# Attention weights and their x in float16 halves, and transposes moved from TensorE to transposing DMAs

## The reference

```
x = x + layernorm(attn(layernorm(x), W_qkv, W_out))
x = x + layernorm(ffn(layernorm(x), w_gate_up, w_proj))

attn:  qkv = x @ W_qkv.T                       # W_qkv 1536 x 512, 16 heads of 32
       q, k = phi(q), phi(k)                   # phi(x) = elu(x) + 1
       out = q * cumsum(k * v) / (q * cumsum(k) + 1e-9)   # elementwise, along the tokens
       return out @ W_out.T * 32 ** -0.5       # W_out 512 x 512
ffn:   weights rounded to scale * {-1, 0, 1} in groups of 64 (4096 x 512 and 512 x 2048)
       gate, up = split(x @ wq_gu.T);  h = silu(gate) * up
       return rms_norm(h) @ wq_p.T
```

## Time and profile before

| | us |
|---|---|
| median of 2 runs (1126.14 and 1129.27) | 1127.7 |
| span of the profiled execution | 1126.3 |
| PE busy in it | 1090.9 (97%) |
| DVE busy | 759.4 (67%) |
| POOL busy | 518.8 (46%) |
| ACT busy | 465.2 (41%) |

### The profile page before, as it was taken

One profiled execution on the slowest core, in us unless ns is written; L12 is line 12 of the kernel. 1 busy time (PEld: TensorE's weight loads), 2 busy tenths in 40 slices (PEclk: granted clock), 3 DMA queues, 4 the chain that ended last, 5 costly groups with the idle time before them and its releaser, 6 DMA issues. The chain is left out here.

```text
span 1126.3 us, 14647 instructions
## 1 busy us (share of the span) xinstructions
PE 1090.9 (97%) x5376; PEld 656.7 (58%) x5376; DVE 759.4 (67%) x1220; ACT 465.2 (41%) x788; POOL 518.8 (46%) x474
## 2 busy tenths in 40 slices
PE   7998889999999999999999999999999999999997
PEld 6876455554566864468544774458644685544443
DVE  5999989875678697448862588427873479445323
ACT  5546576664522134422443224432444234423433
POOL 1567687987352444425424254414344254234322
PEclk9998999999999999999999999999999999999999
DMA  7021333110030210002100210002100020100101
GB/s 273 17 75 39 112 107 118 57 29 1 1 113 1 75 38 1 1 1 75 38 1 1 76 38 1 1 1 75 38 1 1 1 75 1 38 1 1 38 1 38
DMA packets 29256, 44.99 MB, mean 40 GB/s; under 512 B 1536, under 2 KB 9728, under 8 KB 29184
## 3 DMA queue, kind: packets, MB, share of 16 engines
q1 hardware_dynamic: 29184, 44.05, 12.2%
HBM read 34.60 MB, written 9.44 MB: 39 GB/s over the span
## 5 line engine op out<-in xcount | busy, mean ns | idle before, releaser
L546 PE MATMUL bank<-x3t,wgu_t 128*128 128x512 f16 x1536 | 348.6, 381 | 2.2 <-ACT ht L952 1.6
L546 PEld LDWEIGHTS bank<-x3t,wgu_t 128*128 128x128 bf16 x1536 | 149.1, 98 | 181.2 <-issue 4.3
L1287 POOL TENSOR_TENSOR acc<-acc,ht 128x512 f32<-128x512 f32 x90 | 114.6, 1274 | 252.0 <-ACT ht L993 251.1
L582 PE MATMUL bank<-wproj_t,hid 128*128 128x512 bf16 x872 | 203.4, 379 | 1.7 <-ACT wproj_t L873 1.7
L1658 DVE TENSOR_TENSOR ht<-ht,bank 128x512 f32<-128x512 f32 x112 | 76.0, 678 | 141.6 <-PE bank L546 124.6
L527 PE MATMUL bank<-xnt,wqkv_hi 128*128 128x512 f32 x672 | 168.0, 392 | 0.0
L582 PEld LDWEIGHTS bank<-wproj_t,hid 128*128 128x128 f16 x872 | 85.1, 98 | 102.1 <-issue 2.6
L527 PEld LDWEIGHTS bank<-xnt,wqkv_hi 128*128 128x128 f32 x672 | 125.2, 188 | 25.9 <-issue 0.2
L980 ACT ACTIVATE hid<-ht 128x512 f16<-128x512 f32 x109 | 68.7, 630 | 164.9 <-DVE ht L1658 164.8
L1664 DVE TENSOR_TENSOR hid<-ht,hid 128x512 f16<-128x512 f32 x109 | 83.0, 761 | 65.7 <-ACT hid L980 65.2
L1233 POOL TENSOR_TENSOR tk<-tq,ts 128x512 f32<-128x512 f32 x28 | 52.4, 1871 | 125.8 <-DVE ts L1569 98.5
(11 more groups left out here) (189 smaller groups left out, 1561.0 us busy)
## 6 DMA issues: line engine op xcount, KB each, us to landing
raw_q<-in_L_ffn_w_gate_up_dram SPq DMA_DIRECT2D x32, 256.0 KB, 2.8
xn<-in_L_attn_x_dram SPq DMA_DIRECT2D x7, 1024.0 KB, 5.3
out_dram<-xn SPq DMA_DIRECT2D x7, 1024.0 KB, 8.8
x<-in_L_attn_x_dram SPq DMA_DIRECT2D x6, 1024.0 KB, 6.6
raw_q<-in_L_ffn_w_proj_dram SPq DMA_DIRECT2D x16, 256.0 KB, 2.8
raw_a<-in_L_attn_W_qkv_dram SPq DMA_DIRECT2D x12, 256.0 KB, 5.5
xn<-in_L_attn_x_dram SPq DMA_DIRECT2D x4, 256.0 KB, 3.1
raw_out<-in_L_attn_W_out_dram SPq DMA_DIRECT2D x4, 256.0 KB, 6.6
```

The lines of the kernel that those rows point to most:

```text
L546: last = pe.matmul(bank[:], wgu_t[:, k, first_row:first_row + P], x[:, part, k], start=(n == 0), stop=(n == 2 * KD - 1))
L582: last = pe.matmul(bank[:], hid_of(f, part, k)[:, t * P:(t + 1) * P], wproj_t[:, k], start=(k == 0 and part == 0), stop=(k == MT - 1 and p ...
L1287: pool.tensor_tensor(acc[:], acc[:], ht_of(f)[:, m % 2], ALU.add).then_inc(q["acc_done"], 1)
```

## The change

- `wqkv_hi`, `wqkv_lo`, `xnt` and `xnt_b` become float16. W_qkv's rows are scaled by powers of two first: DVE finds each row's largest magnitude (`weight_peak`), makes the power from it in six tiny instructions (`weight_power`: `enlarge` and its inverse `reduce`). ACT's `weight_hi` and DVE's `weight_lo` write the scaled parts in row layout (`wsplit`), and `reduce` goes as a scale into the relu, the exp and the product that read the groups' banks.
- `turn_weights`, `turn_x` and `turn_x3` on SP are transposing DMAs, SBUF to SBUF: 8 of 128x12x128 for W_qkv (hi and lo of four tiles), 2 of 128x16x128 (512 KB each, hi and lo) for x of each of the chunks 1 to 7 and for x3 of each of the 8 chunks. ACT (`x_hi`, `x3_hi`) and DVE (`x_lo`, `x3_lo`) now split `xn` itself, in row layout, into `xs` and `x3s`, ahead of the DMA.
- PE keeps the transposes of x of chunk 0 (16) and of W_out (16). 288 others go: 48 of W_qkv, 112 of x, 128 of x3.
- 13 of the 16 loads of raw weight tiles are issued by ACT now, after the last tile of x has come, and ahead of all other work of ACT.
- A unit of hidden tile 0 waits for x3's high part at its first matmul and for the low one at its fifth. The low part of x for a group is waited for with the high one at group 0.
- FFN weight batches no longer share memory with `xnt`.

The step lists are also written in another way (`run_steps`, `close` and the class `Step` are gone). The diff, cut to its core, with its hunks in the order tensors, SP, PE, ACT, DVE:

```
-        wqkv_hi = sb("wqkv_hi", [P, KD, 3 * D], F32R)
+        wqkv_hi = sb("wqkv_hi", [P, KD, 3, KD, P], FP16)
-        xnt = sb("xnt", [P, 2, KD, N], F32R)
+        xnt = sb("xnt", [P, 2, KD, N], FP16)
+        xs = sb("xs", [P, 2, KD, NT, P], FP16)
+        x3s = sb("x3s", [P, 2, KD, NT, P], FP16)
...
+            def turn_weights(*tiles):
+                for j in tiles:
+                    for part, (w, done, ready) in enumerate(((wqkv_hi, wt_hi, w_hi), (wqkv_lo, wt_lo, w_lo))):
+                        sp.wait_ge(ready, 3 * (j + 1))
+                        sp.dma_start_transpose(w[:, j].rearrange("p q k n -> p (q k) n"),
+                                               wsplit[j % 2][:, part].rearrange("p q d -> p (q d)")).then_inc(done[j], 16)
+            def turn(x, split, part, ready, count, done):
+                sp.wait_ge(ready, count)
+                sp.dma_start_transpose(x[:, part].rearrange("p k (t n) -> p (k t) n", n=P),
+                                       split[:, part].rearrange("p k t n -> p (k t n)")).then_inc(done, 16)
+            def turn_x(c):
+                if c == 1:
+                    sp.wait_ge(w_hi, NG)
+                    sp.wait_ge(w_lo, NG)
+                elif c > 2:
+                    sp.wait_ge(qkv_done, NG * c)
+                turn(xnt_of(c), xs, 0, xs_hi, NT * c, xt_hi)
+                turn(xnt_of(c), xs, 1, xs_lo, NT * c, xt_lo)
...
+            def start():
+                load_first_x(0, 1, 2, 3), load_raw(0, 1, 2), turn_weights(0), load_x(1), turn_weights(1, 2, 3), load_half(0, 1, 2)
+                load_residual(0), load_half(3, 4, 5), turn_x(1), load_half(6, 7, 8, 9, 10, 11, 12, 13), turn_x3(0)
...
+            def step(s):
+                turn_x3(s - 1), next_x(s + 1), turn_x(s + 1), next_residual(s), store(s - 1)
...
             def gate_up_unit(f, bank, m, which):
+                    if m == 0 and k == 0:
+                        pe.wait_ge(x3t_lo if part else x3t_hi, 16 * (f + 1))
...
+            def load_raw(*tiles):
+                act.wait_ge(x0_in[NT - 1], 16)
...
+                    act.dma_start(raw_a[j][:, part], rows).then_inc(raw_a_in[r], 16)
+            def x_hi(c, *tiles):
...
+                    act.activation(xs[:, 0, :, t], rows_of(xn, t), ACT.Copy).then_inc(xs_hi, 1)
...
             def start():
-                norm_tile(0, 0, 1, 2, 3), split_weight(0), split_x(0, 0, 1, 2, 3), split_weight(1, 2, 3, 4, 5, 6, 7)
+                load_raw(3, 4, 5, 6, 7, 8, 9, 10, 11, 12, 13, 14, 15), norm_tile(0, 0, 1, 2, 3), weight_hi(0, 0, 1, 2), split_first_x(0, 1, 2, 3), weight_hi(1, 0, 1, 2)
...
+            def weight_lo(j, *parts):
...
+                    dve.scalar_tensor_tensor(wsplit[j % 2][:, 1, part], raw_a[j][:, part], enlarge[:, j, part:part + 1],
+                                             wsplit[j % 2][:, 0, part], ALU.mult, ALU.subtract).then_inc(w_lo, 1)
+            def x3_lo(f, *tiles):
...
+                    dve.tensor_tensor(x3s[:, 1, :, t], rows_of(xn, t), x3s[:, 0, :, t], ALU.subtract).then_inc(x3s_lo, 1)
...
             def start():
-                split_weight(0), split_x(0, 0, 1, 2, 3), split_weight(1, 2, 3, 4, 5, 6), stats_tile("1", 1, 0, 1), feature_q(0, 0)
+                weight_peak(0), weight_power(0, 0, 1), split_first_x(0, 1, 2, 3), weight_lo(0, 0, 1, 2), weight_peak(1, 2, 3)
+                weight_power(1, 1, KD), weight_lo(1, 0, 1, 2), stats_tile("1", 1, 0, 1), feature_q(0, 0)
...
-                split_weight(7, 8), feature_k(0, 1), split_weight(9, 10, 11), feature_q(0, 1), split_weight(12)
+                weight_lo(2, 0, 1, 2), feature_k(0, 1), weight_lo(3, 0, 1, 2), feature_q(0, 1), split_out(0)
```

More of the change, by code:

```diff
@@ L332, in wait_group_read, with rows_of, x3t_of @@
                 eng.wait_ge(phi_act, at(2 * KD, c, 2 * j + part))
[L334 to L347, removed]
+        def rows_of(x, t):
+            return x[:, t].rearrange("p (k n) -> p k n", n=P)
+        def x3t_of(f):
+            return {1: x3t_b, NC - 1: x3t_last}.get(f, x3t)
         def half_source(b, i):
@@ L365, in own_instruction, with single_of, x1_of, att_bank @@
             eng.sem_inc(passed_pool if eng is nc.gpsimd else passed_dve, 1)
[L367 to L382, removed]
+        def single_of(f):
+            return EARLY_OUT if f == NC - 2 else MT
+        def x1_of(f):
+            return {1: x1_b, NC - 1: x1_last}.get(f, x1)
+        def att_bank(c, t):
+            return ps[{1: 4 + t, NC - 1: 2 + t % 2}.get(c, t)]
+        def final_bank(f, t):
+            return ps[t if f == 1 else 4 + t]
+        def final_base(f):
+            return x1_last if f == NC - 1 else x1
         block = ctx.enter_context(nc.Block())
@@ L387, in _, with turn_x3, load_half @@
         def _(sp):
[L388 to L400, removed]
+            def turn_weights(*tiles):
[16 more added lines that the diff above has]
+                turn(xnt_of(c), xs, 1, xs_lo, NT * c, xt_lo)
+            def turn_x3(f):
+                if f > 1 and f < NC - 1:
+                    sp.wait_ge(FF_MAIN["gate_done"], MT * ffn(f)[1])
+                    sp.wait_ge(FF_MAIN["up_done"], MT * ffn(f)[1])
+                turn(x3t_of(f), x3s, 0, x3s_hi, NT * (f + 1), x3t_hi)
+                turn(x3t_of(f), x3s, 1, x3s_lo, NT * (f + 1), x3t_lo)
+            def load_half(*halves):
+                for n in halves:
                     if n >= RAW:
@@ L461, in _ @@
-            run_steps(sp, step)
+            next_residual(2), store(1)
+            for s in range(3, NC - 1):
+                step(s)
+            last_steps()
             sp.wait_ge(stored, 16 * (NC - 1 + NT))
@@ new lines, in project, with project_rest, gate_unit, up_unit @@
+                    last.then_inc(q["pr_done"], 1)
+            def project_rest(f, first, *tiles):
+                for t in tiles:
+                    for k in range(first, MT):
+                        if t == 0:
+                            wait_hid(f, k)
+                        last = project_tile(f, k, t)
+                    last.then_inc(tile_done, 1)
+            def gate_unit(f, *tiles):
+                for m in tiles:
+                    unit(f, m, 0)
+            def up_unit(f, *tiles):
+                for m in tiles:
+                    unit(f, m, 1)
@@ L769, in project_att_at, with project_att @@
[L769 removed]
+            def project_att(s, *tiles):
                 for t in tiles:
@@ new lines, in weight_hi, with split_out @@
+            def weight_hi(j, *parts):
+                for part in parts:
+                    act.wait_ge(w_enlarge, 1 if j == 0 else 2)
+                    act.wait_ge(raw_a_in[3 * j + part], 16)
+                    if j >= 2 and part == 0:
+                        act.wait_ge(wt_hi[j - 2], 16)
+                    act.activation(wsplit[j % 2][:, 0, part], raw_a[j][:, part], ACT.Copy,
+                                   scale=enlarge[:, j, part:part + 1]).then_inc(w_hi, 1)
+            def split_out(*tiles):
+                for r in tiles:
@@ L1855, in _ @@
             start()
-            run_steps(dve, step)
+            for s in range(3, NC - 1):
+                step(s)
+            last_steps()
 _INS = ['L0_attn_x', 'L0_attn_W_qkv', 'L0_attn_W_out', 'L0_ffn_w_gate_up', 'L0_ffn_w_proj']
```

1098 lines of the change are left out of this document (497 added, 601 removed).

## The result

The changed kernel takes 1177.15 us (two runs, 1176.25 and 1178.05) against 1127.7: 1.0438 times the time before, interval 1.0399 to 1.0477. The profiled execution has a span of 1176.3 us, 50.0 more than the one before.

The account below looks back on a forecast made before the run. The prediction took PE as the bound, busy 1090.9 of 1126.3 us. It summed 1126.3 + 31.5 (start) - 10.1 (steps) = 1147.7, plus 1.4 from profiled span to median, to 1149.1 us; range 1105 to 1196.

Parts of the forecast that it names:

- the forecast's own case: Whole kernel: X of 4 to 6.5 gives 1135 to 1163 us, at chance 0.43.
- X: Time from a transposing DMA's issue until its 512 KB have landed: taken as 5.3 us, with 2.8 and 8.8 in the range.
- What PE saves: On PE: float16 groups at 0.2159 us a matmul and transposes of x, x3 and W_qkv gone, gross 42.4 us.
- The start: Chunks 0 to 3: late group 0, group 6 and chunk 1 (+22.5), then FFN 0 and chunks 2 and 3; sum +31.5 us.
- three falls: Chunks 0 and 1: PE returns from a wait at a lower clock, +1.1 us each time.
- The steps: Steps 3 to 7 and FFN 7's x3: float16 and removed transposes, less the x3 stall, sum -10.1 us.
- It stands X - 2.5 = 2.8 us in each step: At gate/up's fifth matmul in each step, PE waits 2.8 us for x3's transposing DMA.
- I price no fall here: Behind the steps' x3 stall: no lower clock counted; five falls would add 5.5 us, held by the range.
- B: Rival for the whole kernel: X small (2.8 to 4) but the start late, 1122 to 1135 us; chance 0.19.
- C: Rival at steps' x3 and start: paired DMAs share engines, second lands late, X 7 to 9, slower (1168 at 7); chance 0.22.
- A: Rival for the whole kernel: the DMAs hide and the start is not late, 1085 to 1105 us; chance 0.13.
- D: Rival for the groups: float16 no faster, since their matmul count is the same, +12.5 us, 1162; chance 0.03.

Follow-up runs that it names:

- e4: The kernel before, with W_qkv's and the attention x's two parts in float16, no power-of-two scaling, all transposes left on PE: 1118.15 us, 0.9923.
- h1: e4 plus x of chunks 4 to 7 split in row layout and transposed by DMAs; start, W_qkv and x3 stay on PE: 1110.75 us, 0.9860.
- e2: The changed kernel with all 16 loads of raw weight tiles issued by SP, none by ACT: 1170.2 us.
- e1: The changed kernel with the transposing DMAs of chunk 1's x moved on SP ahead of the loads of halves 3 to 5: 1174.6 us.
- h2: h1 plus x3 of chunks 2 to 6 transposed by DMAs, split where the change splits it: 1127.9 us, 1.0011.
- e5: The changed kernel with GpSimd's products of blocks 1 to 3 held in steps 3 to 7 until DVE has split x3: 1168.5 us.
- h3: h2 with GpSimd's products of blocks 1 to 3 held until DVE has split x3: 1120.7 us, 0.9948.

## Why the prediction was wrong

The forecast was 1149.1, +21.4 us on the profiled span; +50.0 was measured. The time lies inside the stated range, but outside the forecast's own case, and the cause was not the one that I gave the slow end (X of 7 to 9): that the range holds it is luck.

**X.** Taken 5.3, measured 4.2 for x3, 4.6 for x, 4.0 and 3.8 for W_qkv. By 11 us per us of X this alone should have brought the time down by some 10. What I mis-sized is the issue: 0.5 us in my sum, 1.3 to 3.6 in the trace. Two issued back to back cost 7.5 us at chunk 1, where I had 6.3: from the first issue at 78.44, on SP's timeline,

```profile
78.44 5.20 SPq L411 DMA_TRANSPOSE xnt_b<-xs  x2
```

to PE's start at 85.91. The estimate of 21 us for 16 blocks, made from the figure of the Trainium skill ("VectorE: DVE Perf Modes", The three transpose paths) for one block, is contradicted by the 4.2 to 4.6; the Trainium skill's "as fast as regular DMAs" ("Advanced Engine Details and Errata", X-Bar Transpose (TRN2)) came nearer: in this profile plain loads of 256 KB took 2.9 and of 1 MB 6.0.

**What PE saves.** Right: 0.216 us a matmul (e4: 1.5 us a step), and 1.66 for x (h1).

**The start, +31.5 in the sum, +43.7 by group 3 of chunk 3** (428.60 for 384.86). The chain was right in its links: ACT's issues (e2), group 6 at 53.7 (49.5 said), chunk 1 last. Its ends were 1.4, 4.2 and 7.2 us late. Three terms were mis-sized. ACT's way to the norm: its first issue went out at 6.81, not at 5.3, and the 13 took 6.9 us, so the norm began at 15.0 instead of 13.0, which X of 3.8 paid back in part at group 0. The clock: I priced three falls at 1.1 us. Measured, 12 matmuls after the wait take 5.07 us at group 0, 4.57 at group 6, 5.1 at chunks 1 and 3 and 4.3 at chunk 2, against 2.59, and chunk 1's second group is slow as well: 1.7 to 2.9 us for each of five waits, some 11.5 in all where I had 3.3. And DVE's splits with both operands in SBUF: 2.99 us for the three of W_qkv's tile 2 and 2.29 for two of x, 1.6 and 1.9 times what I took from the earlier trace rows. The places of the earlier trace rows came out about as sized at chunks 2 and 3 (+3.0 and +4.0, said 3.5 and 3.7); FFN 0 stood twice, 4.6 and 3.5 us, but was late by only 3.7 more at the next place, FFN 1. One link was half right: the load of half 5 does hold chunk 1's x, but taking it away gives 5 us (e1), not the 10 that my theory had, since DVE's last split, behind two reciprocals, holds it next.

**The steps, -10.1 in the sum, +6.3 measured** (43.7 to 50.0). This is the step that failed, in two terms: "It stands X - 2.5 = 2.8 us in each step" and "I price no fall here". The place was right, and the arrival of PE too (31.2 us after group 0 said, 31.1 measured). The first term: the duration of the splits was carried over from an instruction that read PSUM to one that reads `xn` in SBUF while GpSimd works there: 4.79 for 2.48. With X = 4.2 the stall is then 2.8 - 1.1 + 2.3 = 4.0; 3.7 was measured. The second term is the larger: I had weighed the fall of the clock, at 1.1 us for each step, and priced it at nothing. It fell in every step and cost 2.8, 1.3, 1.7, 2.9 and 2.9 us, 11.6 in all, of the 16.4 by which the sum of the steps was off. In step 4 the 3.7 and the 1.3, with 0.2 at the edges of the waits, make 5.2 lost against 4.9 gained: +0.3 instead of -2.1, and the later ones +0.9 and +2.0, nearly all of the difference by the clock.

**The clock in the whole.** The stretches at 0.50 cost 21 us more than before (half of 52.7 - 10.7), and 3.3 were in my sum: 17.7 of the 28.6 us that the forecast missed. The slow splits, the late norm and the long issues make up the rest, and more, against which the smaller X counts.

**The rivals.** B had X nearly right and the time wrong; C had the time by luck and not the cause, since X is not 7 to 9. No rival had the mechanism. A fell with the late start, D with e4.

Two things stay open: why the clock falls behind one wait of 3.5 us and not behind the next (h2), and how much of the start each of W_qkv and x of chunk 1 takes, since only the start as a whole was put back on PE.

## What to carry to other kernels

A transpose that leaves the bottleneck engine pays only where its whole new path (split, issue, landing) is covered: x's had 30 us of cover and gave all of its 1.66 us a step; x3's had none and cost 5.1 us a step (h2 against h1) for the 1.66 that it saved. A new wait on the engine that sets the time costs more than its length: price the lower clock behind it, from rows that show it. Here it was the largest term of the miss, and a change that cut one wait of 3.5 us into two of under 2 gained most of its time by the clock (e5, h3). When the source of an operation moves from PSUM to SBUF, take its duration from a row with both operands in SBUF and with GpSimd at work. And before counting a saving on the bound engine, ask which engine reaches the next join last once it is faster: here ACT's silu, which the waits of the profile before named once, with 1.6 us.

## What the runs showed of the hardware

- DVE and GpSimd slow each other where both work on SBUF: four float16 subtractions 4.79 us together with GpSimd, 2.50 alone; GpSimd's product 2.04 and 1.27. The Trainium skill ("Advanced Engine Details and Errata", GPSIMD Details) states this for DVE instructions with two SBUF inputs, since the two engines share a read and a write interface; the traces agree (2.50 to 4.79).
- A transposing DMA from SBUF to SBUF in float16 took 3.8 to 4.0 us for 12 blocks of 128x128 and 4.2 to 4.6 for 16 (medians), so a third more blocks took 0.2 to 0.8 us more. Its issue kept SP 1.3 to 3.6 us in the changed kernel, where the median of a plain one was 0.4.
- After ten waits of 2.7 to 15 us in the changed kernel (five ahead of groups in the start, five for x3 in the steps) PE worked at a granted clock of 0.50, 1.2 GHz, and each cost 1.3 to 2.9 us beyond itself. In h2 two waits of 3.5 and 3.8 us had no such stretch behind them, and in e5 and h3 none of the waits in the steps, of up to 1.8 us, had one.
